# Mixture of experts in a decoder megakernel: three of eight token tiles of the weighted sum go from VectorE to GpSimd, and one of eight output evictions from ScalarE to VectorE

## What is computed

```python
router_logits = x2d @ gate_w
routing_weights = jax.nn.softmax(router_logits, axis=-1)
routing_weights, selected_experts = jax.lax.top_k(routing_weights, TOP_K)
routing_weights = routing_weights / jnp.sum(routing_weights, axis=-1, keepdims=True)
...
layer_w0 = jax.lax.ragged_dot(sorted_inputs, gate_k, group_sizes, preferred_element_type=jnp.bfloat16)
layer_w1 = jax.lax.ragged_dot(sorted_inputs, up_k, group_sizes, preferred_element_type=jnp.bfloat16)
intermediate = jax.nn.silu(layer_w0) * layer_w1
expert_out = jax.lax.ragged_dot(intermediate, down_k, group_sizes, preferred_element_type=jnp.bfloat16)
...
out = jnp.einsum('tke,tk->te', unsorted, routing_weights.astype(jnp.float32))
```

## Time and profile before

| what | value |
|---|---|
| median of 3 runs | 2390.32 us (2388.5 to 2397.09) |
| the profiled execution: its own time / its span | 2401.34 us / 2399.2 us |
| TensorE clock granted over the span | 0.857 of full speed |
| busy share of the span: PE, DVE, ACT, POOL | 83%, 73%, 56%, 18% |
| the stage of the experts in the span | about 566 to 945 us |
| first and last L1280 | 592.5 and 941.4 us |

### The profile page before, as it was taken

One profiled execution on the slowest core, in us unless ns is written; L12 is line 12 of the kernel. 1 busy time (PEld: TensorE's weight loads), 2 busy tenths in 40 slices (PEclk: granted clock), 3 DMA queues, 4 the chain that ended last, 5 costly groups with the idle time before them and its releaser, 6 DMA issues. The chain is left out here.

```text
span 2399.2 us, 34791 instructions
## 1 busy us (share of the span) xinstructions
PE 1985.9 (83%) x11353; PEld 1305.1 (54%) x11353; DVE 1748.1 (73%) x3892; ACT 1344.8 (56%) x2644; POOL 422.0 (18%) x587
## 2 busy tenths in 40 slices
PE   6999999986777675885877996598999999958978
PEld 4776767664333333562753353465667676723545
DVE  6888888777999998756996874666636464668734
ACT  5777777765898887355444365423333333253641
POOL 2333333321111110101732000300101010110000
PEclk8999999997776876795678798599999999977989
DMA  6000000002212100502503100150000000042010
GB/s 225 1 4 1 4 1 4 1 1 100 57 43 60 60 1 23 161 3 43 108 2 80 48 3 18 51 203 2 2 2 1 1 1 1 1 121 67 16 37 18
DMA packets 62030, 94.52 MB, mean 39 GB/s; under 512 B 9403, under 2 KB 48139, under 8 KB 59415
## 3 DMA queue, kind: packets, MB, share of 16 engines
q1 hardware_dynamic: 58604, 87.81, 12.0%
q0 software_dynamic: 1728, 4.22, 0.8%
q10 hardware_dynamic: 1536, 0.49, 0.1%
HBM read 80.53 MB, written 10.49 MB: 38 GB/s over the span
## 5 line engine op out<-in xcount | busy, mean ns | idle before, releaser
L1280 DVE SCALAR_TENSOR_TENSOR moe_acc<-moee_eo,moe_wsel,moe_acc 128x256 f32<-128x256 bf16 x512 | 226.4, 512 | 0.6
L887 DVE SCALAR_TENSOR_TENSOR l_acc<-l_px,l0w_chan,l_acc 128x253 f32<-128x253 f32 (+2 forms) x288 | 137.5, 477 | 80.6 <-POOL l_acc L855 80.1
L1185 PE MATMUL moee_po<-moee_db,moee_hb 96*128 96x256 bf16 (+1 forms) x768 | 137.2, 347 | 23.2 <-ACT moee_eo L1212 18.3
L1212 ACT CAST moee_eo<-moee_po 128x512 bf16<-128x512 f32 x256 | 133.2, 595 | 38.5 <-PE moee_po L1185 36.4
L1170 PE MATMUL moee_pu<-moe_xb,moee_wb 128*128 128x512 bf16 x192 | 71.9, 515 | 77.2 <-DVE moee_ub L1269 77.2
L1185 PEld LDWEIGHTS moee_po<-moee_db,moee_hb 96*128 96x128 bf16 (+1 forms) x768 | 92.3, 122 | 75.0 <-ACT moee_eo L1212 23.5
L1724 ACT ACTIVATE l3xa_ex<-l3xa_pS 128x512 f32<-128x512 f32 x128 | 74.1, 605 | 81.8 <-PE l3xa_pS L1637 77.4
L1724 ACT ACTIVATE l2a_ex<-l2a_pS 128x512 f32<-128x512 f32 x128 | 73.9, 605 | 80.1 <-PE l2a_pS L1637 75.6
L560 PE MATMUL l_pz<-xT,l0w_w_in 128*128 128x256 f32 x384 | 111.4, 413 | 2.5 <-DVE l_sz L935 2.5
L560 PE MATMUL l_px<-xT,l0w_w_in 128*128 128x256 f32 x384 | 103.5, 393 | 4.3 <-DVE l_acc L887 4.3
L3118 ACT COPY l3b_bc<-l3b_pbc 128x512 f32<-128x512 f32 x48 | 28.1, 586 | 137.1 <-PE l3b_pbc L3068 137.1
(11 more groups left out here) (624 smaller groups left out, 5548.7 us busy)
## 6 DMA issues: line engine op xcount, KB each, us to landing
moe_wf<-in_moe_up SPq DMA_DIRECT2D x48, 256.0 KB, 3.2
l3w_w_in<-in_l_w_in SPq DMA_DIRECT2D x1, 8224.0 KB, 26.1
m1b_bc<-bc_rows SPq DMA_DIRECT2D x16, 512.0 KB, 11.2
moe_df<-in_moe_down SPq DMA_DIRECT2D x48, 128.0 KB, 3.5
l_qs<-parts_q SPq DMA_DIRECT2D x36, 128.0 KB
l0w_w_in<-in_l_w_in SPq DMA_DIRECT2D x2, 1536.0 KB, 13.1
l0w_w_out<-in_l_w_out SPq DMA_DIRECT2D x1, 3072.0 KB
parts_q<-l_pieces SPq DMA_DIRECT2D x16, 192.0 KB, 2.3
```

What stands on the lines that cost most here:

```text
L887: nc.vector.scalar_tensor_tensor(out=a, in0=px[:, 0:S - (L0_CONV - 1 - c)], scalar=w, in1=a, op0=ALU.mult, op1=ALU.add).then_inc(tap_done, 1)
L1185: last = nc.tensor.matmul(po[:, t, :], hb[rows, j % H, t * P:(t + 1) * P], db[rows, j % H, :], start=(n == 0), stop=(n == len(parts) - 1))
L1212: nc.scalar.copy(eo[:, e % 2, 2 * q:2 * q + 2, :], po[:, 2 * q:2 * q + 2, :]).then_inc(o_read, 1)
L1280: last = nc.vector.scalar_tensor_tensor(out=acc[:, t, :], in0=eo[:, e % 2, t, :], scalar=wsel[:, t, e:e + 1], in1=acc[:, t, :], op0=ALU.mu ...
```

## The change

- GpSimd takes token tiles 5, 6 and 7 of each expert (NV = 5 stay with VectorE). It does them in two instructions of 128x768: a product of `eo` with `wsel` broadcast along the features into the new `prod` (f32), and a sum of `acc` and `prod`. Between the two it waits for its own product, and before the next product for its own sum. It waits for quarters 2 and 3 of `eo`.
- GpSimd's casts are written into the same loop: three units ahead (AHEAD is 3, it was 2), and then one unit's casts per step.
- VectorE evicts quarter 0 of every odd expert from `po` (two of 16 evictions in a group), with a semaphore `o_read_v` of its own; ScalarE skips these.
- `eo` has three buffers (ER), it had two. ScalarE now waits for VectorE's and GpSimd's use of the buffer. The last three tiles are rounded once GpSimd is done.

```diff
--- before.py
+++ after.py
@@ -1085,6 +1085,17 @@
 
         with Stage(nc, "moee") as st:
             R, H, U, LAG = MOE_RING, 9, MOE_N, 3
+            ER, NV = 3, 5
+
+            def by_vector(e, q):
+
+                return e % 2 == 1 and q == 0
+
+            def reads(e, q):
+
+                mine = by_vector(e, q)
+                count = sum(by_vector(a, c) == mine for a in range(e + 1) for c in range(4) if (a, c) <= (e, q))
+                return (o_read_v if mine else o_read), count
             LAST = MOE_E - 1
 
             def before(i):
@@ -1107,7 +1118,8 @@
             ex = st.sbuf("ex", [P, 4, TOK], BF16)
             lx = st.sbuf("lx", [P, 2, TOK])
             hb = st.sbuf("hb", [P, H, TOK], BF16)
-            eo = st.sbuf("eo", [P, 2, NT, D], BF16)
+            eo = st.sbuf("eo", [P, ER, NT, D], BF16)
+            prod = st.sbuf("prod", [P, NT - NV, D])
             accb = st.sbuf("accb", [P, NT, D], BF16)
             prob = st.sbuf("prob", [P, NT, MOE_E])
             rest = st.sbuf("rest", [P, NT, MOE_E])
@@ -1120,9 +1132,9 @@
             logits, v_chain, shifted, prob_done, xb_done, zeroed = st.sem(
                 "logits", "v_chain", "shifted", "prob_done", "xb_done", "zeroed")
             (cast, g_done, u_done, g_read, u_read, exp_done, one_plus, ln_done, inv_done, gated, h_done,
-             o_done, o_read, used, summed, rounded) = st.sem(
+             o_done, o_read, used, summed, rounded, routed, used_p, weighed, o_read_v) = st.sem(
                 "cast", "g_done", "u_done", "g_read", "u_read", "exp_done", "one_plus", "ln_done",
-                "inv_done", "gated", "h_done", "o_done", "o_read", "used", "summed", "rounded")
+                "inv_done", "gated", "h_done", "o_done", "o_read", "used", "summed", "rounded", "routed", "used_p", "weighed", "o_read_v")
             with st.block() as block:
 
                 @block.sync
@@ -1144,12 +1156,29 @@
                         nc.gpsimd.tensor_copy(wb[:, i % R, :, :, :], wf[:, i % R, :, :, :])
                         nc.gpsimd.tensor_copy(db[:, i % H, :], df[:, i % R, :]).then_inc(cast, 1)
 
-                    AHEAD = 2
+                    AHEAD = 3
                     for i in range(AHEAD):
                         cast_weights(i)
                     nc.gpsimd.memset(acc[:, :, :], 0.0).then_inc(zeroed, 1)
-                    for i in range(AHEAD, U):
-                        cast_weights(i)
+                    for i in range(U + LAG):
+                        if i + AHEAD < U:
+                            cast_weights(i + AHEAD)
+                        if i == LAG:
+                            pool.wait_ge(zeroed, 1)
+                            pool.wait_ge(routed, 1)
+                        if i >= LAG:
+                            for e in experts(i - LAG):
+                                if e >= 1:
+                                    pool.wait_ge(used_p, e)
+                                pool.wait_ge(*reads(e, 2))
+                                pool.wait_ge(*reads(e, 3))
+                                nc.gpsimd.tensor_tensor(
+                                    prod[:, :, :], eo[:, e % ER, NV:NT, :],
+                                    wsel[:, NV:NT, e:e + 1].broadcast_to([P, NT - NV, D]), ALU.mult
+                                ).then_inc(weighed, 1)
+                                pool.wait_ge(weighed, e + 1)
+                                nc.gpsimd.tensor_tensor(acc[:, NV:NT, :], acc[:, NV:NT, :], prod[:, :, :], ALU.add
+                                                        ).then_inc(used_p, 1)
 
                 @block.tensor
                 def _(pe):
@@ -1176,7 +1205,7 @@
                             for e in experts(i - LAG):
                                 for q in range(4):
                                     if e >= 1:
-                                        pe.wait_ge(o_read, 4 * (e - 1) + q + 1)
+                                        pe.wait_ge(*reads(e - 1, q))
                                     elif q == 0:
                                         pe.wait_ge(shifted, 1)
                                     for t in range(2 * q, 2 * q + 2):
@@ -1205,11 +1234,14 @@
                                                  scale=-1.0).then_inc(exp_done, 1)
                         if i >= LAG:
                             for e in experts(i - LAG):
-                                if e >= 2:
-                                    act.wait_ge(used, e - 1)
+                                if e >= ER:
+                                    act.wait_ge(used, e - ER + 1)
+                                    act.wait_ge(used_p, e - ER + 1)
                                 for q in range(4):
+                                    if by_vector(e, q):
+                                        continue
                                     act.wait_ge(o_done, 4 * e + q + 1)
-                                    nc.scalar.copy(eo[:, e % 2, 2 * q:2 * q + 2, :],
+                                    nc.scalar.copy(eo[:, e % ER, 2 * q:2 * q + 2, :],
                                                    po[:, 2 * q:2 * q + 2, :]).then_inc(o_read, 1)
                         if 1 <= i <= U:
                             j = i - 1
@@ -1221,7 +1253,10 @@
                             nc.scalar.activation(ex[:, j % 4, :], lx[:, j % 2, :], ACT.Exp,
                                                  scale=-1.0).then_inc(inv_done, 1)
                     for t in range(NT):
-                        act.wait_ge(summed, t + 1)
+                        if t < NV:
+                            act.wait_ge(summed, t + 1)
+                        elif t == NV:
+                            act.wait_ge(used_p, MOE_E)
                         nc.scalar.copy(accb[:, t, :], acc[:, t, :]).then_inc(rounded, 1)
 
                 @block.vector
@@ -1256,7 +1291,9 @@
                             link(nc.vector.tensor_tensor(prob[:, :, :], prob[:, :, :], across(small[:, 3, :, None]),
                                                          ALU.mult))
                             link(nc.vector.tensor_scalar(rest[:, :, :], rest[:, :, :], 0.0, None, ALU.is_lt))
-                            link(nc.vector.tensor_tensor(wsel[:, :, :], prob[:, :, :], rest[:, :, :], ALU.mult))
+                            nc.vector.tensor_tensor(wsel[:, :, :], prob[:, :, :], rest[:, :, :], ALU.mult
+                                                    ).then_inc(routed, 1)
+                            dve.wait_ge(routed, 1)
                             dve.wait_ge(zeroed, 1)
 
                     for i in range(U + LAG):
@@ -1275,10 +1312,15 @@
                             for e in experts(i - LAG):
                                 if e >= 1:
                                     dve.wait_ge(used, e)
-                                for t in range(NT):
-                                    dve.wait_ge(o_read, 4 * e + t // 2 + 1)
+                                if by_vector(e, 0):
+                                    if e >= ER:
+                                        dve.wait_ge(used_p, e - ER + 1)
+                                    dve.wait_ge(o_done, 4 * e + 1)
+                                    nc.vector.tensor_copy(eo[:, e % ER, 0:2, :], po[:, 0:2, :]).then_inc(o_read_v, 1)
+                                for t in range(NV):
+                                    dve.wait_ge(*reads(e, t // 2))
                                     last = nc.vector.scalar_tensor_tensor(
-                                        out=acc[:, t, :], in0=eo[:, e % 2, t, :], scalar=wsel[:, t, e:e + 1],
+                                        out=acc[:, t, :], in0=eo[:, e % ER, t, :], scalar=wsel[:, t, e:e + 1],
                                         in1=acc[:, t, :], op0=ALU.mult, op1=ALU.add)
                                     if e == LAST:
                                         last.then_inc(summed, 1)
```

## The result

The change makes the kernel slower: 2471.19 us median of four runs (2459.04 to 2473.24) against 2393.69 of four (2388.5 to 2397.09), a ratio of 1.0315 with a 95% interval of 1.0274 to 1.0357. The forecast was 2469 us, 3.3% slower. The profiled execution of the change took 2469.58 us, 68.2 more than the one of before.

The account below looks back on a forecast made before the run. DVE was taken to bound the stage: 17.5 us a group alone, plus 13.8 held out by POOL, less 4.0 hidden, 27.3 against 22.5. Over 16 groups plus 2 us that adds 79 us: 2469 us, 3.3% slower, range 2395 to 2535.

Parts of the forecast that it names:

- The bound: DVE's time per group sets the stage's time, 22.5 us before the change, with ACT next at 20.0.
- DVE without POOL, 17.5 us: DVE's undisturbed time per group after the change: 20 sums, two new evictions and 8.3 us for the rest.
- POOL's instructions: Eight new 128x768 products and sums per group, 1.81 us each; 1.8 to 2.3 us in the trace as a sign.
- What POOL costs DVE: Time POOL holds DVE out per group: 12.3 us from eight new instructions plus 1.5 from casts, 13.8, less 4.0 hidden.
- 0.15 and 0.12: Microseconds taken off a POOL instruction's length for its cost to DVE: 0.15 not held, 0.12 of DVE's instruction hidden.
- End of the stage, +2 us: After the last eviction POOL still has a product and a sum, 3.6 us, adding 2 us once.
- The sum, 79 us: Total added time: 16 groups x (27.3 - 22.5) us, plus 2 us at the stage's end.
- ACT, DVE's wait for PE, casts: nothing: ACT at 19.0 us a group, DVE's new wait on o_done and casts three units ahead were each set at no cost.
- Rival 1: POOL's long instructions do not hold DVE out: a group of some 20 us, 2352 us, faster; chance 0.14.
- The scans: DVE instructions in the profile, taken to read two SBUF tiles, not lengthened beside POOL's products; cited as evidence against holding out.
- Rival 2: POOL's product is cheap, 0.82 us: a group of 23.3 us, 2405 us; chance 0.10.
- Rival 3: POOL's product is dear, 2.7 us: a group of 30.9 us, 2527 us; chance 0.06.

Follow-up runs that it names:

- e3: The change with GpSimd's product and sum replaced by scratch-buffer fills of 1640 and 2120 columns, tiles 5 to 7 left out: 2381.26 us, 0.9944 of the kernel before.
- e4: The bench: kernel before with added stages, POOL repeating one instruction and DVE another, alone and together; sums take 2017 to 2064 ns when they meet a product.
- e1: The change with ScalarE making all evictions again: 2482.12 us, 1.0353 of the kernel before.
- e10: The kernel before with one more wait, so that GpSimd's casts start when VectorE goes on to read pu from PSUM: 2391.21 us, 0.9981.
- e11: The change with fills for GpSimd's product and sum (tiles 5 to 7 left out) and all evictions by ScalarE: 2393.38 us, 1.0001 of the kernel before.
- e9: The kernel before with a second bench, of operand forms for POOL's products of 1024 columns; scans beside them take up to 4471 ns.

## Why the prediction was right

- **The bound.** DVE paced the stage before and paces it after. Right.
- **DVE without POOL, 17.5 us.** In e3 DVE's busy time is 17.9 a group. Right within 0.4.
- **POOL's instructions.** The sum was put at 1.81 and is 1.86 us at its shortest. The product was put at 1.81 too, and takes 1.47, outside the 1.8 to 2.3 us named as a sign. Here the step "since both operands are read for all 768 columns" failed: e4 shows that the broadcast along the features makes it cheaper (1.47 us with either type, against 1.79 and 1.64).
- **What POOL costs DVE.** Forecast 1.54 per instruction, 13.8 a group with the casts. With the lengths as found and the same 0.15 and 0.12 it would be 4 x (1.20 + 1.60) + 1.5 = 12.7. Measured from mean lengths against those of e3, where next to nothing is held out, DVE's instructions grow by (789 - 479) x 20 for the sums, (1140 - 692) x 3 and (772 - 689) x 3 for the products and (729 - 418) x 3 for the `tensor_scalar`: 8.7 us. The difference of 4.0 is what hid, as forecast; the count from the trace gives 4.0 too. The forecast's 27.3 a group was 0.6 too high: 1.1 too much here, by the product, less the 0.4 of the point above.
- **End of the stage, +2 us.** Wrong and small: POOL's last sum ended before DVE's last, at 1011.4 against 1012.5 us, because the last units are held out as well. From DVE's last sum to the end of the stage it is 2.7 us in both kernels.
- **The sum, 79 us.** The profiled executions differ by 68.2, the medians by 77.5. Part of the agreement of the medians is luck: by the terms it should have been ten less.
- **ACT, DVE's wait for PE, casts: nothing.** Right in the time. The eviction was even a gain of 11 us beside GpSimd's part (e1); I had it only as 1.2 us of PSUM reads under which POOL can work.
- **Rival 1** (no holding out, 2352) fell. The Trainium skill ("SBUF — State Buffer", Who interferes with whom) has it that a DVE instruction with two SBUF inputs contends with a GpSimd instruction that reads SBUF, but not with one that only writes it. Both halves agree with the pairs that were run: sums take 2017 to 2064 ns beside products and 480 beside fills. The scans were no case against it: that they read two tiles of SBUF like the sums was false, since one of the two lies in PSUM, and the prediction's "By that rule the scans should have waited" misread the case. Had I looked at where the operand is kept, rival 1 would have had nothing for it. The bench adds what the page's words on issue order leave open: when both queues are full, the engines take strict turns. Rival 1's number was wrong too: e3, with next to nothing held out, shows 2381 and a group of 21.4, not the 20 that I took from busy times.
- **Rival 2** (a cheap product) was a third right: 1.47, neither 0.82 nor 1.81. **Rival 3** has nothing for it.

## What to carry to other kernels

An idle GpSimd is no free VectorE. What cost VectorE 1.2 us (the sums of three tiles) took GpSimd 3.3 in two instructions, and all but some 0.3 us of each was time in which VectorE's instructions with two SBUF inputs and its bf16 `tensor_scalar` would stand still (the bench: 1.54 of 1.79). Only the part that lay beside VectorE's PSUM reads was free, 4.0 us a group here. Before weighing a pair in a trace against such a rule, look up in which memory each operand lies; and before summing a gain from busy times, ask which chain of waits comes next, since here three different ways to free VectorE (e3, e10, e11) ended at 21.4 to 22.2 us a group, with VectorE busy for 16.7 to 21.1.

## What the runs showed of the hardware that was not expected

- Strict turns, whole instructions, for long ones too (e4): f32 products of 1024 columns on VectorE take 2.82 us beside POOL's of 768 columns; alone the two take 1.22 and 1.79.
- A GpSimd fill, which reads nothing, leaves the two-input sums alone (480 ns) but holds out the bf16 `tensor_scalar`, to 2099 to 2159 ns, in turns as well (e4). In e3 no fill fell on one, and they average 418 ns.
- On GpSimd a product with an operand broadcast along the last dimension takes 1.47 us for 768 columns (e4) and 1.90 for 1024 (e9); two plain f32 tiles take 1.79 and 2.34.
